# Experts of two layers: second products ahead of the next group's first, back transposes in the same step, the rows added by the experts

## The chip, the cores and the metric

The kernel runs on one core of one Trainium2 chip, in one launch. TensorE (PE in the profile, with PEld for its weight loads) multiplies, VectorE (DVE), ScalarE (ACT) and GpSimd (POOL) work on the results, and SyncE (SP) issues most DMAs. The metric is device time in microseconds (us); lower is better. Engines wait for each other by semaphores, and every wait and its order is written by hand.

## What is computed

Four transformer layers with normalisation behind each sum, on 16 sequences of 256 tokens of width 128, all in float32:

```python
x = _layernorm(x + _L0_attn_ref(x, ...), axis=-1)
x = _layernorm(x + _L0_ffn_ref(x, ...), axis=-1)    # 8 experts of width 512, each token takes 2
x = _layernorm(x + _L1_attn_ref(x, ...), axis=-1)   # one head, softmax over the queries
...
x = _layernorm(x + _L3_attn_ref(x, ...), axis=-1)   # linear attention
x = _layernorm(x + _L3_ffn_ref(x, ...), axis=-1)    # 16 experts, each token takes 1, capacity 320
```

In layer 0 a token's result is the sum of its two experts' outputs, each weighted by the softmax of the two router logits, so that the two weights add up to 1. In layer 3 a token goes to one expert, weighted by its probability; the tokens beyond an expert's 320 places get nothing from the layer, so that x alone is normalised.

## The kernel before

**Staging.** The stages follow each other: attention and routing of layer 0; the experts of layer 0; the combination of their results, in the same sweep as the attention of layer 1; mixing, attention, mixing; the linear attention and routing of layer 3; the experts of layer 3; the last stage, which combines, normalises and stores. The activations of all tokens stay on chip in `xg`.

**How a stage is ordered.** A stage is a `sweep(eng, lags, step)` on each engine. In step s, `at(k)` is the item s - k, so `at(0)` is the newest item and `at(3)` one that began three steps ago. On an engine the code runs in the order in which it is written. Items rotate through four slots (`q.slot`), some tiles through two. `wait_apart` waits for a semaphore; `q.back(3)` as a count says that item n - 4 is through.

**Experts (`experts_*`).** Tokens have been scattered into a table in memory, sorted by expert, each row with its destination row (column D) and its weight (column D + 1). An item is a group: 256 rows of one expert in layer 0 (T = 256, 40 groups), or one expert's 320 places in layer 3 (T = 320, 16 groups). SyncE loads its rows into `xe` (L1508; for T = 320 also L1511) and the expert's weights into `we` (L1478). On TensorE a step holds, in this order: the row transposes of item s (L1523, `xe` to `p0`), the first products of item s - 1 (L1530, four chunks into `pt` and `pm`), the second products of item s - 2 (L1536, four chunks into `po0`), and the back transposes of item s - 3 (L1543, `yt` to `po1`). ScalarE applies the GELU to each chunk of the first products (L1555, `he`). VectorE copies the transposed rows (L1569, `xet`), adds the bias (L1574, or a plain copy, L1577: `yt`), copies weight and destination (L1580 and L1581: `w_row`, `to_row`), and scales the result (L1589, `ye`). GpSimd scatters `ye` to memory with one indirect DMA for each 128 rows (L1613). The semaphores carry the names of the tiles: `he_ps` counts first products, `he_sb` GELUs, `yt_ps` second products, `ye_ps` back transposes.

**Behind the experts of layer 0.** Each token has two result rows. `combine_sync` waits for all scatters, then loads both for a sequence into `yr` (L1627, slot free when the sum of item s - 4 is made). `combine_vector` makes two sums (L1651: first result plus `xg`; L1655: plus the second result, into `mixed.res`), then the statistics (L319, L322); GpSimd takes the root (L328, L331, `norm_rstd`), and VectorE normalises into `xg` (L340). In the same steps, six items behind, VectorE does its part of layer 1's attention (`single_vector`); TensorE's part is `single_tensor`, whose products L796 wait for a normalisation by VectorE.

**Layer 3.** The linear attention leaves its normalised rows in `rows3`; SyncE copies them to `xg` on chip (L998), while GpSimd scatters them to the experts' table. The result table `yd3` in memory is filled with zeros early on (L1694), since dropped tokens have no result. The last stage loads one result row per token (L1627), adds `xg` (L1655), normalises and stores (L1664).

## Time and profile before

| | |
|---|---|
| three runs, median (lowest to highest) | 1377.04 us (1372.11 to 1378.55) |
| the profiled execution, whole | 1373.05 us |
| its span in the trace | 1371.3 us, granted TensorE clock 0.89 on average |
| busy share of the span | PE 79%, DVE 61%, ACT 47%, POOL 27% |
| experts of layer 0: first row transposes to the end of the last scatter | 362.4 to 530 us |
| combination of layer 0 with layer 1's attention | from 530.1 us |
| experts of layer 3: first row transposes to the end of the last scatter | 1232.4 to 1332 us |
| last stage | 1332 to 1371.3 us |

The shares are averages over stages of different kinds; what a change in one stage is worth is read from that stage: which engine has no idle time there, and which wait ends last. In a row of the trace that is ordered by time, the first number is the start, the second the duration (of all instructions of the row, if it ends in x2 or more), and in brackets the idle time before it with the engine and the tile that ended it. A float32 product counts as two MATMUL instructions.

### The profile page before, as it was taken

How to read it: one execution, taken by the hardware profiler on the slowest of the kernel's cores; microseconds unless marked ns; L12 is line 12 of the kernel's file. 1: busy time of each engine (PE TensorE's matmuls, PEld its weight loads, DVE VectorE, ACT ScalarE, POOL GpSimd, SP SyncE). 2: the span in 40 equal slices, each digit the busy share in tenths (PEclk: the TensorE clock that was granted, in tenths of full speed). 3: DMA queues.
4: the chain of work that ended last, by engine and by line, in shares of the span. 5: the costliest groups of instructions: out<-in, count | busy, mean ns of one | idle time of the engine just before them, and what ended most of it. 6: DMA issues, size and time to landing. Idle time of an engine off the chain costs nothing. (4 is left out here: it accounts for less than half of the span.)

```text
span 1371.3 us, 33015 instructions
## 1 busy us (share of the span) xinstructions
PE 1080.8 (79%) x9594; PEld 733.9 (54%) x9623; DVE 832.8 (61%) x3269; ACT 643.8 (47%) x1505; POOL 377.1 (27%) x602
## 2 busy tenths in 40 slices
PE   5989989886499994777779989998877798819950
PEld 2334444433388883676645545555566677716730
DVE  3788899985233334875645666667445677742327
ACT  2577777763344441554326656666633432204310
POOL 4012332235345444332200000000012133342554
PEclk9999999997699997999968999999999855559985
DMA  5222332312567677210032222221010011133523
GB/s 160 76 74 80 82 89 83 81 34 81 153 197 203 205 208 233 89 35 31 25 85 61 62 62 51 61 62 35 18 34 32 24 44 40 32 108 105 170 70 103
DMA packets 146579, 119.27 MB, mean 87 GB/s; under 512 B 16657, under 2 KB 134674, under 8 KB 146322
## 3 DMA queue, kind: packets, MB, share of 16 engines
q1 hardware_dynamic: 136912, 100.73, 25.8%
q0 software_dynamic: 7168, 14.37, 3.1%
q10 hardware_dynamic: 2370, 2.56, 0.7%
q8 instruction: 68, 1.11, 0.3%
q14 instruction: 61, 0.50, 0.1%
HBM read 47.26 MB, written 23.41 MB: 52 GB/s over the span
## 5 line engine op out<-in xcount | busy, mean ns | idle before, releaser
L655 DVE TENSOR_REDUCE mx<-pm 128x2 f32<-128x512 f32 (+1 forms) x512 | 304.8, 619 | 123.5 <-PE pm L450 74.2
L599 ACT ACTIVATE ex<-pt 128x512 f32<-128x512 f32 (+1 forms) x512 | 269.4, 547 | 163.4 <-PE pt L443 85.8
L328 POOL TENSOR_SCALAR ve<-mv 128x2 f32<-128x2 f32 x96 | 22.1, 230 | 661.3 <-DVE mv L322 660.8
L437 PE MATMUL pm<-ks,qs 64*128 64x256 bf16 (+1 forms) x1024 | 172.8, 259 | 8.3 <-DVE mx L655 5.2
L443 PE MATMUL pt<-qs,ks 64*128 64x256 bf16 (+1 forms) x1024 | 164.7, 250 | 0.6 <-ACT ex L599 0.3
L1613 POOL DMA_INDIRECT result<-ye,to_row x128 | 122.5, 957 | 151.6 <-issue 108.2
L474 PE MATMUL po<-ex,va 128*32 128x256 f32 (+1 forms) x2048 | 153.0, 371 | 6.0 <-issue 6.0
L437 PEld LDWEIGHTS pm<-ks,qs 64*128 64x128 bf16 x1024 | 74.2, 99 | 88.0 <-issue 53.4
L1536 PE MATMUL po<-he,we 128*128 128x256 f32 (+1 forms) x448 | 112.9, 395 | 0.6 <-DVE yt L1574 0.4
L424 PE MATMUL pm<-hide_q,half_id 64*128 64x256 bf16 (+1 forms) x512 | 89.1, 260 | 16.1 <-DVE mx L655 9.3
L1536 PEld LDWEIGHTS po<-he,we 128*128 128x128 f32 x448 | 85.0, 190 | 19.3 <-DVE yt L1574 0.6
L429 PE MATMUL pt<-hide_k,half_id 64*128 64x256 bf16 (+1 forms) x512 | 85.7, 252 | 1.3 <-ACT ex L599 0.9
L1574 DVE TENSOR_SCALAR yt<-po,we 128x256 f32<-128x256 f32 x40 | 19.4, 484 | 104.2 <-PE po L1536 104.2
L1555 ACT ACTIVATE he<-pt,we 128x256 f32<-128x256 f32 x80 | 36.1, 473 | 94.0 <-PE pt L1530 94.0
L443 PEld LDWEIGHTS pt<-qs,ks 64*128 64x128 bf16 x1024 | 70.6, 96 | 8.6 <-issue 6.7
L340 DVE TENSOR_SCALAR xg<-res,mv,rstd 128x128 f32<-128x128 f32 (+1 forms) x128 | 39.2, 349 | 56.6 <-POOL rstd L331 55.5
L1373 POOL DMA_INDIRECT sorted<-xr,place x64 | 63.8, 997 | 26.5 <-POOL xr L1367 13.4
L331 POOL TENSOR_TENSOR rstd<-ve,half 128x2 f32<-128x2 f32 x96 | 68.8, 717 | 8.0
L424 PEld LDWEIGHTS pm<-hide_q,half_id 64*128 64x128 bf16 x512 | 30.6, 96 | 74.5 <-issue 51.4
L311 ACT COPY xt<-p 128x256 f32<-128x256 f32 x96 | 35.4, 368 | 73.4 <-PE p L307 73.3
L1530 PE MATMUL pt<-xet,we 128*128 128x256 f32 (+1 forms) x224 | 64.8, 413 | 0.0
L1530 PE MATMUL pm<-xet,we 128*128 128x256 f32 (+1 forms) x224 | 62.5, 402 | 0.0
(294 smaller groups left out, 2460.4 us busy)
## 6 DMA issues: line engine op xcount, KB each, us to landing
we<-in_pack SPq DMA_DIRECT2D x40, 514.5 KB
xs<-xg SPq DMA_DIRECT2D x96, 128.0 KB, 2.0
qs<-parts SPq DMA_DIRECT2D x192, 64.0 KB
ks<-parts SPq DMA_DIRECT2D x192, 64.0 KB
we<-in_pack SPq DMA_DIRECT2D x16, 512.0 KB
xe<-sorted SPq DMA_DIRECT2D x56, 132.0 KB, 2.2
yr<-result SPq DMA_DIRECT2D x48, 128.0 KB, 2.2
xr<-xg SPq DMA_DIRECT2D x32, 128.0 KB, 2.3
```

The lines of the kernel that those rows point to most:

```text
L331: nc.gpsimd.tensor_tensor(of.rstd[q.slot][:, :, :], of.ve[q.slot][:, :, :], half[:, :].unsqueeze(2), ALU.pow).then_inc(of.ln_rs, 1)
L424: pe.matmul(dst, half_id[rows_m, lo // HALF, :], hide_q[rows_m, lo // HALF:lo // HALF + 1, lo:P].to_broadcast([HALF, 2, P - lo]), start=fi ...
L429: pe.matmul(dst, half_id[rows_t, 1 - lo // HALF, :], hide_k[rows_t, 1 - lo // HALF:2 - lo // HALF, 0:P - lo].to_broadcast([HALF, 2, P - lo ...
L437: last_m = pe.matmul(mine[:, e * S + k0:e * S + k1], queries, keys[:, k0:k1], start=not causal, stop=e == 1 or not causal)
L443: last_t = pe.matmul(theirs[:, e * S + k0:e * S + k1], keys, queries[:, k0:k1], start=not causal, stop=e == 1 or not causal)
L474: last = pe.matmul(po[32 * i:32 * i + 32, b // 2, c0 + lo:c0 + S], va[q.slot][:, kt, 4 * b + i, :], ex[j % 2][:, i, lo:S], start=(kt == 0) ...
L599: nc.scalar.activation(ex[j % 2][:, :, :].rearrange("p (e g) k -> p g e k", g=2)[:, 1 - u, :, lo:S], pt[:, u, :].rearrange("p (b k) -> p b ...
L655: nc.vector.tensor_reduce(mx[q.slot % 2][:, qt, u, 2 * b:2 * b + 2], pm[:, u, :].rearrange("p (b k) -> p b k", k=S)[:, :, 0:hi], AX.X, ALU ...
L1373: pool.indirect_dma_start(out=rows, out_offset=bass.IndirectOffsetOnAxis(ap=place[q.slot][:, i, t:t + 1], axis=0), in_=tile[:, t, :], in_o ...
L1530: pe.matmul(hb[c][:, 0:T], we[q.slot][:, c * P:c * P + P], xet[q.slot % 2][:, 0:T], start=True, stop=True).then_inc(he_ps, 1)
L1536: last = pe.matmul(po0[:, 0:T], we[q.slot][:, W2_AT + c * D:W2_AT + c * D + D], he[q.slot % 2][:, c, 0:T], start=(c == 0), stop=(c == FC - 1))
L1613: pool.indirect_dma_start(out=rows, out_offset=bass.IndirectOffsetOnAxis(ap=to_row[q.slot][0:m, i:i + 1], axis=0), in_=ye[q.slot][0:m, i, ...
```

## The change

- **Order on TensorE.** A step of the experts is now: row transposes of item s, second products of item s - 2, first products of item s - 1, back transposes of item s - 2. So the second products come ahead of the next group's first, and their results are transposed back in the same step; every engine's sweep has three lags in place of four.
- **The experts add the rows.** The scatter no longer writes the scaled result alone. In layer 3, `ye` becomes x + weight * result, in one operation for each 128 rows; in layer 0 it becomes 0.5 * x + weight * result in two operations on 256 rows, since each token has two rows that are summed. `w_row` goes: the weight is read from `xe`. Since `xe` is read until `ye` is made, the load of new rows waits for `ye_sb` instead of `to_row_sb`.
- **Combination.** In layer 0 one sum of the two result rows is left. In layer 3 SyncE writes the normalised rows of the linear attention to `yd3` in place of `xg`, and the scatters of the experts overwrite the rows of the tokens that were kept (GpSimd waits for those writes); the fill with zeros goes. The last stage loads each sequence's rows from `yd3` straight into `mixed.res` (`last_sync`), takes the statistics and normalises two steps later (`last_vector`), without a sum. The load of item s waits until item s - 4 is normalised.

```diff
@@ norm_stats
-        def norm_stats(dve, q, done, of=None, bank=None):
+        def norm_stats(dve, q, done, of=None, bank=None, loaded=False):
...
-            dve.wait_ge(of.res_sb, done + q.n + 1)
+            if not loaded:
+                dve.wait_ge(of.res_sb, done + q.n + 1)
@@ linear_sync
-                    sp.dma_start(xg[:, bass.ds(2 * q.n, 2), :], rows3[q.slot][:, :, 0:D]).then_inc(rows_moved[q.slot], 16)
+                    sp.dma_start(yd3[bass.ds(SPARE + q.n * S, S), :].rearrange("(t p) d -> p t d", p=P),
+                                 rows3[q.slot][:, :, 0:D]).then_inc(rows_moved[q.slot], 16)
@@ experts_sync
-                    wait_apart(sp, to_row_sb, a + q.back(3), passed)
+                    wait_apart(sp, ye_sb, a + q.back(3), passed)
@@ experts_tensor
                     last.then_inc(xet_ps, 1)
+                if (q := at(2)):
+                    wait(pe, yt_sb, a + q.n)
+                    pe.wait_ge(he_sb, 4 * (a + q.n + 1))
+                    for c in range(FC):
+                        last = pe.matmul(po0[:, 0:T], we[q.slot][:, W2_AT + c * D:W2_AT + c * D + D],
+                                         he[q.slot % 2][:, c, 0:T], start=(c == 0), stop=(c == FC - 1))
+                    last.then_inc(yt_ps, 1)
                 if (q := at(1)):
...
                 if (q := at(2)):
-                    wait(pe, yt_sb, a + q.n)
-                    pe.wait_ge(he_sb, 4 * (a + q.n + 1))
-                    for c in range(FC):
-                        last = pe.matmul(po0[:, 0:T], we[q.slot][:, W2_AT + c * D:W2_AT + c * D + D],
-                                         he[q.slot % 2][:, c, 0:T], start=(c == 0), stop=(c == FC - 1))
-                    last.then_inc(yt_ps, 1)
-                if (q := at(3)):
                     pe.wait_ge(yt_sb, a + q.n + 1)
                     wait(pe, ye_sb, a + q.n)
...
-            sweep(pe, 4, step, n, lead=0 if a else 1)
+            sweep(pe, 3, step, n, lead=0 if a else 1)
@@ experts_vector
                     for i, j, m in whole:
-                        nc.vector.tensor_copy(w_row[q.slot][0:m, i:j, :], xe[q.slot][0:m, i:j, D + 1:D + 2]).then_inc(w_row_sb, 1)
                         last = nc.vector.tensor_tensor(to_row[q.slot][0:m, i:j].unsqueeze(2), xe[q.slot][0:m, i:j, D:D + 1],
...
-                if (q := at(3)):
                     dve.wait_ge(ye_ps, a + q.n + 1)
-                    dve.wait_ge(w_row_sb, a + len(whole) * (q.n + 1))
                     wait(dve, grp_out[q.slot], outs + 16 * k * q.turn)
-                    for i, j, m in whole:
-                        last = nc.vector.tensor_tensor(ye[q.slot][0:m, i:j, :],
-                                                       po1[0:m, i * D:j * D].rearrange("p (t d) -> p t d", d=D),
-                                                       w_row[q.slot][0:m, i:j, :].to_broadcast([m, j - i, D]), ALU.mult)
+                    if biased:
+                        nc.vector.tensor_tensor(ye[q.slot][:, 0:2, :], po1[:, 0:2 * D].rearrange("p (t d) -> p t d", d=D),
+                                                xe[q.slot][:, 0:2, D + 1:D + 2].to_broadcast([P, 2, D]),
+                                                ALU.mult).then_inc(scaled_sb, 1)
+                        dve.wait_ge(scaled_sb, q.n + 1)
...
+                        last = nc.vector.scalar_tensor_tensor(ye[q.slot][:, 0:2, :], xe[q.slot][:, 0:2, 0:D], 0.5,
+                                                              ye[q.slot][:, 0:2, :], ALU.mult, ALU.add)
+                    else:
+                        for i, m in pieces(T):
+                            last = nc.vector.scalar_tensor_tensor(ye[q.slot][0:m, i:i + 1, :],
+                                                                  po1[0:m, i * D:i * D + D].unsqueeze(1),
+                                                                  xe[q.slot][0:m, i, D + 1:D + 2],
+                                                                  xe[q.slot][0:m, i:i + 1, 0:D], ALU.mult, ALU.add)
                     last.then_inc(ye_sb, 1)
@@ experts_pool
-                pool.wait_ge(zeroed, 48)
+                for s in rows_moved:
+                    pool.wait_ge(s, 48 * (SEQS // SLOTS))
...
-                if (q := at(3)):
+                if (q := at(2)):
@@ combine_vector
                 if (q := at(2)):
-                    dve.wait_ge(gathered[q.slot], got // SLOTS + 16 * choices * (q.turn + 1))
-                    src = xg[:, bass.ds(2 * q.n, 2), :]
-                    if choices == 2:
-                        nc.vector.tensor_tensor(part[q.slot % 2][:, :, :], yr[q.slot][:, :, 0, :], src,
-                                                ALU.add).then_inc(part_sb, 1)
-                        dve.wait_ge(part_sb, q.n + 1)
-                        src = part[q.slot % 2][:, :, :]
-                    nc.vector.tensor_tensor(mixed.res[q.slot][:, :, :], yr[q.slot][:, :, choices - 1, :], src,
+                    dve.wait_ge(gathered[q.slot], 32 * (q.turn + 1))
+                    nc.vector.tensor_tensor(mixed.res[q.slot][:, :, :], yr[q.slot][:, :, 0, :], yr[q.slot][:, :, 1, :],
                                             ALU.add).then_inc(mixed.res_sb, 1)
@@ store_out becomes last_sync
+            def step(at):
+                if (q := at(0)):
+                    wait_apart(sp, mixed.ln_x, 2 * (n + q.back(3)), passed)
+                    sp.dma_start(mixed.res[q.slot][:, :, :],
+                                 yd3[bass.ds(SPARE + q.n * S, S), :].rearrange("(t p) d -> p t d", p=P)
+                                 ).then_inc(gathered[q.slot], 16)
+                if (q := at(4)):
+                    wait_apart(sp, mixed.ln_x, 2 * (n + q.n + 1), passed)
                     sp.dma_start(out[bass.ds(2 * q.n, 2)].rearrange("t p d -> p t d"),
                                  xg[:, bass.ds(2 * q.n, 2), :]).then_inc(out_done, 16)
-            combine_sync(sp, n, 1, yd3, OUTS0 + OUTS3, 7, then)
+            sweep(sp, 5, step)
@@ last_vector (new)
+        def last_vector(dve, n, got):
+            def step(at):
+                if (q := at(0)):
+                    wait_apart(dve, gathered[q.slot], got // SLOTS + 16 * (q.turn + 1), passed)
+                    norm_stats(dve, q, n, mixed, loaded=True)
+                if (q := at(2)):
+                    norm_apply(dve, q, n, mixed)
+            sweep(dve, 3, step)
@@ sync block
-            sp.dma_start(yd3[SPARE:SPARE + SEQS * S, :].rearrange("n d -> (n d)").rearrange("(e p k) -> p e k", p=P, e=SEQS),
-                         zt[:, 0:2 * D].unsqueeze(1).to_broadcast([P, SEQS, 2 * D])).then_inc(zeroed, 16)
@@ vector block
-            for s in rows_moved:
-                dve.wait_ge(s, 48 * (N // SLOTS))
-            combine_vector(dve, N, 1, 32 * N)
+            last_vector(dve, N, 32 * N)
```

TensorE, before, the step that holds the first back transposes of layer 0's experts (`p0` to `po` are banks of results, `xe3` is slot 3 of the rows, `he1` of two the GELUs of item 1):

```order
L1523 MATMUL p0<-ident,xe3 128x128 [waits rows_in_sb3,xet_sb]
L1523 MATMUL p0<-ident,xe3 128x128
L1530 MATMUL pt<-xet0,we2 128x256 [waits he_sb,weights_in2,xet_sb]
L1530 MATMUL pt<-xet0,we2 128x256 [waits he_sb]
L1530 MATMUL pm<-xet0,we2 128x256 [waits he_sb] x2
L1536 MATMUL po<-he1,we1 128x256 [waits he_sb,yt_sb]
L1536 MATMUL po<-he1,we1 128x256 x3
L1543 MATMUL po<-ident,yt0 128x128 [waits yt_sb]
L1543 MATMUL po<-ident,yt0 128x128
```

TensorE, the same place in the change:

```order
L1523 MATMUL p0<-ident,xe2 128x128 [waits rows_in_sb2,xet_sb]
L1523 MATMUL p0<-ident,xe2 128x128
L1529 MATMUL po<-he0,we0 128x256 [waits he_sb]
L1529 MATMUL po<-he0,we0 128x256 x3
L1537 MATMUL pt<-xet1,we1 128x256 [waits he_sb,weights_in1,xet_sb]
L1537 MATMUL pt<-xet1,we1 128x256 [waits he_sb]
L1537 MATMUL pm<-xet1,we1 128x256 [waits he_sb] x2
L1543 MATMUL po<-ident,yt0 128x128 [waits yt_sb]
L1543 MATMUL po<-ident,yt0 128x128
```

The second products (`he0`) have moved ahead of the first products of the next group (`xet1`), and the back transposes of item 0 (`yt0`) follow one step earlier, behind the first products of item 1 instead of those of item 2.

SyncE, before, the last stage's loop (a load, then a store of another sequence):

```order
L1627 ISA [waits res_sb_m]
L1627 DMA yr2<-result3 128x2x128
L1663 ISA
L1664 ISA [waits ln_x_m]
L1664 DMA out_x<-xg 128x2x128
```

SyncE, the same loop in the change:

```order
L1668 ISA [waits ln_x_m]
L1668 DMA res_m0<-result3 128x2x128
L1673 ISA [waits ln_x_m]
L1673 DMA out_x<-xg 128x2x128
L110 ISA
```

The load now has `res_m` as its target and waits for `ln_x_m`, which counts normalisations, where it waited for `res_sb_m`, which counts sums.

## Rows read from the trace of the kernel before

**Rows 1.** Busy time by stretch: length; PE, PEld, DVE, ACT, POOL; clock, DMA share, GB/s

```profile
402.00:442.00 40.00, 40.00 (x208) 35.27 (x207) 13.19 (x51) 17.68 (x40) 20.31 (x21) 1.00 0.71 202
560.00:575.00 15.00, 11.08 (x75) 9.99 (x75) 13.82 (x54) 8.45 (x27) 5.74 (x13) 1.00 0.25 73
```

**Rows 2.** Order of time (start us, us, engine), one step in layer 0's experts

```profile
403.10 1.03 PE L1530 MATMUL pt<-xet,we 128*128 128x256 f32 x4
403.40 0.42 DVE L1589 TENSOR_TENSOR ye<-po,w_row 128x256 f32<-128x256 f32 x1
403.73 0.91 ACT L1555 ACTIVATE he<-pt,we 128x256 f32<-128x256 f32 x2 [2.12 <-PE pt L1530]
404.60 0.91 ACT L1555 ACTIVATE he<-pm,we 128x256 f32<-128x256 f32 x2
404.62 0.97 POOL L1613 DMA_INDIRECT result<-ye,to_row  x1 [1.65 <-issue]
404.83 1.89 PE L1536 MATMUL po<-he,we 128*128 128x256 f32 x8
406.55 0.38 PE L1543 MATMUL po<-ident,yt 128*128 128x128 f32 x2
406.99 1.03 PE L1530 MATMUL pt<-xet,we 128*128 128x256 f32 x4
```

**Rows 3.** Order of time, one step in layer 3's experts

```profile
1255.76 1.34 PE L1530 MATMUL pt<-xet,we 128*128 128x320 f32 x4
1257.68 1.07 ACT L1555 ACTIVATE he<-pm,zero_col 128x320 f32<-128x320 f32 x2
1258.02 2.32 PE L1536 MATMUL po<-he,we 128*128 128x320 f32 x8
1260.17 0.49 PE L1543 MATMUL po<-ident,yt 128*128 128x128 f32 x3
1261.02 1.34 PE L1530 MATMUL pt<-xet,we 128*128 128x320 f32 x4
```

**Rows 4.** Order of time, layer 0's last second products, which wait for yt

```profile
519.42 0.48 DVE L1574 TENSOR_SCALAR yt<-po,we 128x256 f32<-128x256 f32 x1 [2.72 <-PE po L1536]
519.96 1.99 PE L1536 MATMUL po<-he,we 128*128 128x256 f32 x8 [0.36 <-DVE yt L1574]
521.79 0.38 PE L1543 MATMUL po<-ident,yt 128*128 128x128 f32 x2
```

**Rows 5.** Order of time, the last scatter of layer 0's experts

```profile
527.72 0.96 POOL L1613 DMA_INDIRECT result<-ye,to_row  x1 [0.30 <-issue]
```

**Rows 6.** Loads of the experts' rows (xe): time from issue to landing

```profile
DMA to landing us min/median/max: 2.1/2.2/3.8
```

**Rows 7.** Order of time, the last stage: some sums, a load, the last normalisation

```profile
1334.12 0.43 DVE L1655 TENSOR_TENSOR res_m<-yr,xg 128x256 f32<-128x256 f32 x1 [10.97 <-DMA yr<-result]
1350.41 0.42 DVE L1655 TENSOR_TENSOR res_m<-yr,xg 128x256 f32<-128x256 f32 x1
1351.10 0.38 SPq L1627 DMA_DIRECT2D yr<-result  x1
1361.45 0.42 DVE L1655 TENSOR_TENSOR res_m<-yr,xg 128x256 f32<-128x256 f32 x1
1363.96 0.60 DVE L340 TENSOR_SCALAR xg<-res_m,mv_m,rstd_m 128x128 f32<-128x128 f32 x2 [0.75 <-POOL rstd_m L331]
```

**Rows 8.** Order of time, the end of layer 3's experts

```profile
1318.09 2.42 PE L1536 MATMUL po<-he,we 128*128 128x320 f32 x8 [0.25 <-DVE yt L1577]
1329.60 0.90 POOL L1613 DMA_INDIRECT result<-ye,to_row  x1 [0.30 <-issue]
```

**Rows 9.** Order of time, TensorE in layer 1's attention, one sequence to the next

```profile
593.23 0.71 PE L796 MATMUL po<-vn,e 128*128 128x128 f32 x4 [1.15 <-DVE xg L340]
598.47 0.68 PE L796 MATMUL po<-vn,e 128*128 128x128 f32 x4 [1.25 <-DVE xg L340]
603.69 0.68 PE L796 MATMUL po<-vn,e 128*128 128x128 f32 x4 [1.25 <-DVE xg L340]
```

More of the change, by code:

```diff
@@ L779, in post_norm_stack @@
             yr = [sb(f"yr{i}", [P, 2, 2, D], F32, mem) for i in range(SLOTS)]
-            part = [sb(f"part{i}", [P, 2, D], F32, mem) for i in range(2)]
         kq_ps, kq_sb, v1_ps, v1_sb = sem("kq_ps"), sem("kq_sb"), sem("v1_ps"), sem("v1_sb")
@@ L1449, in post_norm_stack @@
         xe = [sb(f"xe{i}", [P, 4, RW]) for i in range(SLOTS)]
-        w_row = [sb(f"w_row{i}", [P, 3, 1]) for i in range(SLOTS)]
         to_row = [sb(f"to_row{i}", [P, 4], U32) for i in range(SLOTS)]
@@ L1557, in step @@
                                              ).then_inc(he_sb, 1)
-            sweep(act, 4, step, n)
+            sweep(act, 3, step, n)
         def experts_vector(dve, a, T, n, biased):
@@ L1615, in step, with combine_sync @@
                             in_=ye[q.slot][0:m, i, :], in_offset=None).then_inc(grp_out[q.slot], 16)
-            sweep(pool, 4, step, n, lead=0 if a else SLOTS)
-        def combine_sync(sp, a, choices, rows, outs_done, lags, then):
+            sweep(pool, 3, step, n, lead=0 if a else SLOTS)
+        def combine_sync(sp, g):
             for s in grp_out:
-                sp.wait_ge(s, outs_done)
+                sp.wait_ge(s, OUTS0)
             def step(at):
                 if (q := at(0)):
-                    wait_apart(sp, mixed.res_sb, a + q.back(3), passed)
-                    for c in range(choices):
+                    wait_apart(sp, mixed.res_sb, q.back(3), passed)
+                    for c in range(2):
                         sp.dma_start(yr[q.slot][:, :, c, :],
-                                     rows[bass.ds(SPARE + c * SEQS * S + q.n * S, S), :].rearrange("(t p) d -> p t d", p=P)
+                                     yd0[bass.ds(SPARE + c * SEQS * S + q.n * S, S), :].rearrange("(t p) d -> p t d", p=P)
                                      ).then_inc(gathered[q.slot], 16)
-                then(at)
-            sweep(sp, lags, step)
+                if (q := at(4)):
+                    load_x(sp, q, g, "mixed")
+            sweep(sp, 5, step)
         def combine_pool(pool, a, then=None):
@@ L1780, in _ @@
             experts_vector(dve, 0, S, NG, True)
-            combine_vector(dve, 0, 2, 0, then=single_vector(dve, N))
+            combine_vector(dve, then=single_vector(dve, N))
             mixing_vector(dve, 0, 2 * N)
```

34 lines of the change are left out of this document (14 added, 20 removed).

## The prediction

> **What bounds the kernel now.** I read the busy time by stretch first, then the order of time inside one step of each stage that the change touches, and last the end of the program. In the experts of layer 0 (from 362 us to about 530 us) TensorE is busy for 40.00 of 40 us at full clock [rows 1]: it is the bound, so the step is what its instructions take. One step goes from a first product at 403.10 to the next at 406.99, 3.89 us [rows 2]: the first products take 1.73 (to 404.83), the second products 1.72 (to 406.55), and the two pairs of transposes 0.44 together. The experts of layer 3 are bound the same way, with 5.26 us (1255.76 to 1261.02) [rows 3]. The combination behind layer 0, which runs with the attention of layer 1, is another case: TensorE is busy for 11.08 of 15 us and VectorE for 13.82 [rows 1]. The last stage is VectorE's and the queues' alone.
>
> **Second products ahead of the next first products, layer 0.** The work on TensorE is the same; what changes is how long ScalarE has between a group's first and second products. Today a whole set of second products and more lies between. In the new order only two pairs of transposes do. First products start at w = 403.10; the first pair of GELUs starts at w + 0.63 and the second pair ends at 404.60 + 0.91 = w + 2.41 [rows 2]. One engine reacts to another's end within 0.06 us: yt ends at 519.42 + 0.48 and TensorE starts at 519.96 [rows 4]. So the second products may start at w + 2.47. TensorE would be ready for them at w + 1.73 + 0.44 = w + 2.17, and waits 0.30. Restarting costs more: the set that waited took 519.96 to 521.79 = 1.83 us [rows 4], against 1.72 in the stream, 0.11 more. Each step becomes 0.41 us longer (4.30). Nothing hides it, since TensorE is the bound. Of 40 groups 37 pay 0.41; the first and the last two, which have one pair of transposes less or a slow start before them, pay about 0.6. That is 15.2 + 1.8 = 17.0 us. At the start of the last second products the old order waits too, for yt: take off about 0.5; one pair of back transposes (0.22) now lies ahead of them, and the restart of that last set (0.11) is counted below: they start 16.6 us later.
>
> The end of the stage gives something back. Before, GpSimd's last scatter starts at 527.72, 7.76 us after the last second products [rows 4, 5], because it works off earlier groups back to back. Now: products 1.83, hand-over 0.2 (w + 0.63 less one product of 0.43), bias 0.48, transposes and hand-over 0.5, scaling and adding the rows 0.9 (one operation more of some 0.42, as the one of 403.40 [rows 2]), then 0.80 to GpSimd (403.40 + 0.42 to 404.62), and one scatter of 0.97 + 0.30: 6.0 us. Gain 1.8. Stage: **+14.8 us**.
>
> Moved with it in the same step: VectorE's extra operation and the lost copies of w_row lie in an engine that is busy for 13.19 of 40 us [rows 1], cost 0. The load of a group's rows now waits for ye instead of to_row. Counted from the start of the back transposes (b): ye ends near b + 1.4, the load lands 2.2 after its issue [rows 6], and the queue reacts by 0.27 (1350.41 + 0.42 to 1351.10, [rows 7]): b + 3.9. The row transposes stand at b + 4.5, and may slip to b + 4.7 since the second products wait anyway. Hidden, with 0.6 us of cover; behind that wait the queue holds the next weights, which are needed some 7 us later.
>
> **The same in layer 3.** First products last 2.26 (1255.76 to 1258.02), second 2.15, so both groups of transposes have 5.26 - 4.41 = 0.85. The last GELUs end at 1257.68 + 1.07 = w + 2.99, usable at w + 3.05; TensorE arrives at w + 3.11 [rows 3]. Cost 0 in the stream, with only 0.06 to spare; if it misses, 15 times 0.15 = 2 us at most. The end again gains: the last second products start at 1318.09 today [rows 8], and 0.9 later in the new order (0.33 for the transposes put ahead, two waits of 0.45 with 0.1 for a restart, less 0.4 of today's wait). Behind them: 2.26 + 0.75 to the back transposes, 0.55 and three operations of a quarter microsecond, 0.8 to GpSimd, two scatters of 1.27: 7.7 us, so the last scatter starts at 1326.7 instead of 1329.60 [rows 8]. **-2.9 us**. The three operations in place of two are bounded by 0.61 (the two of today) and 1.3 (three of 0.42).
>
> **Combination, layer 0.** One of two sums goes, 0.42 + 0.04 us on VectorE for each of 16 sequences, 7.3 us if VectorE's own time set the pace. It doesn't: with the sums the products of the attention start at 593.23 and 598.47 (5.24 apart), and where the sums have run out at 603.69 (5.22 apart), each time after 1.2 us of waiting for VectorE's normalisation [rows 9]. The pace is a ring through TensorE and back, and the sum lies beside it. Only at the start, where VectorE works alone, up to three sums are saved: 0 to 1.35 us; I take **-0.6**, the middle, as the queue there issues three transfers in each step. The zero fill of the result (one DMA) goes and the copy of the rows goes to memory instead of on chip; both end long before anyone waits: 0.
>
> **Last stage.** Today 16 sequences take 1334.12 to 1361.45, 1.82 each [rows 7], with the sum. Without it VectorE needs about 1.35 (1.82 less 0.46). But the rows are now loaded into the buffer that the normalisation still reads, so the load of sequence s waits until s-4 is normalised, and that stands in VectorE's step s-2. From there: 0.27 reaction (1350.41 + 0.42 to 1351.10), 2.2 to land [rows 6], then a step of 1.35. Two steps take 3.82, 1.91 each: **the wait for a load takes the place of the sum**. The first four sequences come from loads issued ahead and end 4.3 us after the first row is there; twelve more take 22.9; the last normalisation 1.4: 28.6 us. Today it is 1363.96 + 0.60 - 1334.12 = 30.4 [rows 7]. **-1.8 us**.
>
> **Sum.** +14.8 - 2.9 - 0.6 - 1.8 = +9.5 us. The profiled execution took 1373.05 us, so 1382.6 for one like it; the median of the three runs shown is 1377.04, 0.3% above it, and the change is small against that spread, so I put it on the median: 1386.5, say **1386**.
>
> **Clock.** In the stretch from 560 to 575 us TensorE idles 1.2 us in every 5.2 and the granted clock stays 1.00 (2.4 GHz) [rows 1], so pauses of 0.3 us in a step of 4.3 should leave it there. The Trainium skill (TensorE: Matmul & The Clock Gate, "A second HAM failure mode: psum-queue depth-cycling") says against this that frequent small pauses between groups of products can make the clock swing between its two levels. By that rule this reordering would be very dear, and the rows of this trace speak against it.
>
> **Rivals.**
> A, the other side: TensorE doesn't wait. If the GELUs were seen by w + 2.17, for which they would have to end 0.30 us earlier than in every step of the trace, the 17.0 us fall away: 9.5 - 17.0 = -7.5, 1369.5. What speaks for it is only that ScalarE is idle for half the time; against it, that its pace is that of the products. 10%.
> B, the row loads come late in layer 0. Landing takes 2.1 to 3.8 us [rows 6]; at 3.8 the rows are there at b + 5.5, 0.8 late. A quarter of the groups late costs 8 us (1394), all of them 30 us. 7%. The Trainium skill (DMA: Bandwidth & Descriptors, "Latency and other measured facts") gives access to HBM as 0.2 us on average and 2 us at high load; by the latter this rival would be the rule. The longest landing of the profile is 1.6 above the median, so it happens, if seldom.
> C, the sum that goes does pay in the combination: up to 16 x 0.46 = 7.3 instead of 0.6, 1379.8. It decides whether the wait before the normalisation begins with VectorE's queue or with TensorE's product. 12%.
> D, in the last stage loads and stores issued together land later, 2.9 instead of 2.2: six pairs of steps, +4.2, 1390.7. 11%.
> E, the clock falls in layer 0: at 1.2 GHz its 3.89 us of products a step double, over 100 us more. 1%.
> The forecast keeps 59%, from 1382 to 1390 with the spread of the runs.
>
> **Numbers.** 0.5% of 1377 is 6.9 us, about what a measurement of this kernel can tell from none. Faster by more: rival A, 8% (2% of it falls within). Within: 2% of A, C, and 16% of the forecast, 30%. Slower: the rest, 62%. The range leaves out A and the worst of B and E: 1376 to 1394.
>
> **What would show it.** In layer 0 TensorE's steps 4.3 us apart with about 0.3 idle before the second products, ended by ScalarE's he; 5.26 in layer 3 with none; the last scatter of layer 0 at about 542 us, some 14 us later; VectorE in the last stage waiting for the load from memory at every second sequence, 1.9 us apart. Steps of 3.9 mean A; TensorE waiting for the rows' DMA before the row transposes means B; products less than 5.1 us apart in the combination mean C. The forecast is wrong if ScalarE's turn is not on the path, or if the queue of the loads sets the step.

## The result and the profile after

The changed kernel takes 1379.69 us (median of 21 runs, 1373.17 to 1384.3) against 1373.88 us for the kernel before, run on the same chip with it (21 runs, 1367.71 to 1378.55): ratio 1.0043, 95% interval 1.003 to 1.0057. It is slower, by 5.8 us or 0.4%; the interval reaches just past 0.5%. The forecast was 1386 and "slower by over 0.5%"; the time lies in the range, the side doesn't. The profiled executions differ by 6.8 us: span 1378.1 after, 1371.3 before.

Where those 6.8 us arise can be followed with marks that both traces have. Each line below is the time from the mark of the line above to its own; the two columns on the right are the second profiled execution of either kernel, on another chip (experiments `g1` and `g2` below).

| stretch, us | before | after | difference | again: before | again: after |
|---|---|---|---|---|---|
| start to the first row transpose of layer 0's experts | 362.38 | 362.02 | -0.36 | 385.48 | 389.88 |
| from there to the end of the last second products | 159.57 | 175.63 | +16.06 | 160.20 | 175.35 |
| to layer 0's last scatter | 5.77 | 4.00 | -1.77 | 5.64 | 4.02 |
| to the last sequence's values in layer 1's attention (L871) | 90.18 | 88.62 | -1.56 | 90.13 | 88.17 |
| to the first row transpose of layer 3's experts | 614.53 | 612.02 | -2.51 | 620.52 | 610.22 |
| to layer 3's last scatter | 97.17 | 94.29 | -2.88 | 96.21 | 93.69 |
| to the end of the last normalisation | 34.96 | 34.83 | -0.13 | 35.11 | 34.55 |

In the first line and the fifth (mixing layers, layer 2, the linear attention of layer 3) the change touches only one fill with zeros and the target of a copy. The others together are +9.7 us, and in the second pair +8.5.

**Layer 0, one step.** Order of time in the changed kernel (start us, us, engine), the rows that answer to [rows 2]:

```profile
421.60 1.03 PE L1537 MATMUL pt<-xet,we 128*128 128x256 f32 x4
...
422.23 0.91 ACT L1555 ACTIVATE he<-pt,we 128x256 f32<-128x256 f32 x2 [2.52 <-PE pt L1537]
...
423.10 0.91 ACT L1555 ACTIVATE he<-pm,we 128x256 f32<-128x256 f32 x2
...
423.33 0.38 PE L1543 MATMUL po<-ident,yt 128*128 128x128 f32 x2
...
423.55 0.38 PE L1523 MATMUL p<-ident,xe 128*128 128x128 f32 x2
...
424.05 1.59 PEld L1529 LDWEIGHTS po<-he,we 128*128 128x128 f32 x8 [0.36 <-ACT he L1555]
424.05 1.99 PE L1529 MATMUL po<-he,we 128*128 128x256 f32 x8
...
425.88 1.03 PE L1537 MATMUL pt<-xet,we 128*128 128x256 f32 x4
```

From 421.60 to 425.88 is 4.28 us, against 3.89. The last GELU ends at 423.10 + 0.91 = 424.01, and 0.04 later the second products start; the weight load had been idle for 0.36. The set then takes 1.83 (424.05 to 425.88), where one in the stream took 1.72 [rows 2]. Busy time by stretch, the rows that answer to [rows 1] (length; PE, PEld, DVE, ACT, POOL; clock, DMA share, GB/s):

```profile
421.00:461.00 40.00, 38.85 (x188) 32.40 (x187) 16.34 (x47) 16.11 (x37) 18.39 (x20) 1.00 0.62 182
574.00:589.00 15.00, 11.99 (x78) 10.79 (x78) 12.63 (x50) 8.29 (x28) 6.03 (x12) 1.00 0.26 82
```

TensorE is no longer busy all the time, and the granted clock stays 1.00 (2.4 GHz) through a pause of 0.36 us in every step. The swing between two clock levels that the Trainium skill describes for another kernel (TensorE: Matmul & The Clock Gate, "A second HAM failure mode: psum-queue depth-cycling") doesn't occur here.

**The ends of both expert stages** (order of time; they answer to [rows 4, 5] and to [rows 8]):

```profile
535.68 1.97 PE L1529 MATMUL po<-he,we 128*128 128x256 f32 x8 [0.44 <-ACT he L1555]
...
541.65 0.96 POOL L1620 DMA_INDIRECT result<-ye,to_row  x1 [0.30 <-issue]
...
1336.58 0.90 POOL L1620 DMA_INDIRECT result<-ye,to_row  x1 [0.31 <-issue]
```

Layer 0's last second products start 15.72 later than before, its last scatter 13.93 later, and 5.97 after those products, against 7.76. In layer 3 the step is unchanged, as these rows show (first products, GELU, second products without a wait, next first products, 5.25 apart):

```profile
1310.05 1.24 PE L1537 MATMUL pt<-xet,we 128*128 128x320 f32 x4
...
1311.87 1.06 ACT L1555 ACTIVATE he<-pm,zero_col 128x320 f32<-128x320 f32 x2
...
1313.08 2.39 PE L1529 MATMUL po<-he,we 128*128 128x320 f32 x8
...
1315.30 0.97 PE L1537 MATMUL pt<-xet,we 128*128 128x320 f32 x3
```

**The last stage**, order of time on SyncE's queue and VectorE; it answers to [rows 7]:

```profile
1353.70 0.39 SPq L1673 DMA_DIRECT2D out_x<-xg  x1
...
1354.47 0.38 SPq L1668 DMA_DIRECT2D res_m<-result  x1
...
1355.12 0.49 DVE L320 BATCH_NORM_STATS2 st_m<-res_m 128x6 f32<-128x128 f32 x2 [1.01 <-DMA res_m<-result]
...
1355.95 0.60 DVE L341 TENSOR_SCALAR xg<-res_m,mv_m,rstd_m 128x128 f32 x2
...
1356.71 0.49 DVE L320 BATCH_NORM_STATS2 st_m<-res_m 128x6 f32<-128x128 f32 x2 [0.16 <-DMA res_m<-result]
1356.81 0.38 SPq L1668 DMA_DIRECT2D res_m<-result  x1
...
1359.02 0.49 DVE L320 BATCH_NORM_STATS2 st_m<-res_m 128x6 f32<-128x128 f32 x2 [0.88 <-DMA res_m<-result]
```

The chain that was forecast is there: a normalisation ends at 1355.95 + 0.60 = 1356.55, the load that waits for it leaves at 1356.81, and VectorE, which has waited 0.88, takes its statistics at 1359.02. Two sequences take 3.90, 1.95 each.

**What the change doesn't touch.** Nearly three microseconds come from a place that the prediction never looks at, the gate of layer 3 in the linear-attention layer. Four steps of that layer are the body of a loop that VectorE runs twice; its branches stand at 1133.5 us (back, for the second pass) and 1171.7 (out). The copy below is the first instruction of the second pass. Order of time, first before, then after:

```profile
1133.22 0.40 DVE L322 BATCH_NORM_AGGREGATE mv<-st 128x2 f32<-128x6 f32 x2
1136.69 0.19 DVE L1226 COPY lg<-pm 128x32 f32<-128x32 f32 x1 [3.07 <-issue]
...
1137.03 0.66 PE L1031 MATMUL pm<-tok,upto 128*128 128x64 f32 x2 [2.80 <-DVE lg L1226]
```

```profile
1146.05 0.40 DVE L323 BATCH_NORM_AGGREGATE mv<-st 128x2 f32<-128x6 f32 x2
1146.77 0.19 DVE L1227 COPY lg<-pm 128x32 f32<-128x32 f32 x1 [0.32 <-issue]
```

"issue" says that the engine waited for nothing that the profile shows. Before, it did so for 3.07 us, after for 0.32. TensorE waits 2.80 for that copy, so the pause is on the path: from the instruction that writes one sequence's `qt` (L1163 before, L1164 after) to the next one, the step that holds it takes 11.82 us before (1130.17 to 1141.99) and 9.06 after (1143.01 to 1152.07). Around it, queues and packets of the kernel before between 1132 and 1138 us (queue, kind: packets, MB, share of the engines):

```profile
q1 hardware_dynamic: 416, 0.26, 14.6%
q0 software_dynamic: 32, 0.07, 3.4%
q14 instruction: 3, 0.02, 1.3%
```

Three packets of instructions, 8 KB each, run in those six microseconds. In the changed kernel there is none between 1138 and 1151 us.

### The profile page after: what moved, and what is told of

Same layout as the page of the kernel before. It is cut to its first block, busy times and chain, and to the rows that moved or that the text cites. A ratio compares the mean times of both kernels' runs of the same rounds, so it can differ in the third digit from the quotient of the medians.

```text
span 1378.1 us, 33009 instructions
## 1 busy us (share of the span) xinstructions
PE 1099.6 (80%) x9623; PEld 734.7 (53%) x9623; DVE 844.1 (61%) x3221; ACT 643.6 (47%) x1505; POOL 374.7 (27%) x602
## 4 chain that ended last, share of the span: by engine, by line
PE 51%; DVE 18%; issue 11%; POOL 9%; ACT 5%; DMA 3%; SPq 1%; DVEq 1%; POOLq 0%; ACTq 0%
PE po L1529 9%; PE po L475 5%; DVE mx L656 4%; PE pm L438 4%; PE pt L1537 4%; PE pm L1537 4%; POOL rstd L332 3%; PE pm L425 3%; DVE xg L341 3%; POOL sorted L1374 3%; PE p L394 3%; ACT he L1555 2%; PE p L537 1%; DVE st L320 1%; PE p L515 1%
## 5 line engine op out<-in xcount | busy, mean ns | idle before, releaser
L1529 PE MATMUL po<-he,we 128*128 128x256 f32 (+1 forms) x448 | 118.6, 407 | 6.8 <-ACT he L1555 2.0
L1529 PEld LDWEIGHTS po<-he,we 128*128 128x128 f32 x448 | 80.7, 190 | 31.7 <-ACT he L1555 14.0
L475 PEld LDWEIGHTS po<-ex,va 128*32 128x32 f32 x2048 | 40.8, 109 | 38.4 <-issue 21.6
```

The lines of the kernel that those rows point to most:

```text
L475: last = pe.matmul(po[32 * i:32 * i + 32, b // 2, c0 + lo:c0 + S], va[q.slot][:, kt, 4 * b + i, :], ex[j % 2][:, i, lo:S], start=(kt == 0) ...
L1529: last = pe.matmul(po0[:, 0:T], we[q.slot][:, W2_AT + c * D:W2_AT + c * D + D], he[q.slot % 2][:, c, 0:T], start=(c == 0), stop=(c == FC - 1))
```

## The experiments

They ran on three other chips, on which the kernel before takes 1400 to 1402 us. The 27 us more lie in the attention of layer 0 and what comes before it (the first line of the table), where the profiles of the experiments are 23 to 33 us longer, whatever the kernel. The other stretches repeat to 1 us or better, half of them to 0.3, except the fifth, which scatters by up to 6. So each experiment is read by its ratio to the kernel before on its own chip, and by its stretches.

### One part alone: the order (f1_order)

```
 (kernel before; experts_tensor)
+                if (q := at(2)):          # second products, ahead of the first ones
+                    ...
                 if (q := at(1)):          # first products
                     ...
-                if (q := at(2)):          # second products
-                    ...
-                if (q := at(3)):          # transposes back
+                if (q := at(2)):
 (experts_vector and experts_pool: ye and the scatter at(2) instead of at(3); no rows added)
```

> The kernel before with one part of the change alone: on TensorE the second products stand ahead of the first ones and the results are transposed back in the same step, and VectorE and GpSimd scatter each group one step earlier; the rows aren't added in the experts, both combination sums and the last stage stay as before. Theory 1 (the order costs layer 0 its step: TensorE waits at the second products for the GELU of the group whose first products have only just ended): step of layer 0 4.28 to 4.30 us against 3.89, with a pause of 0.36 us ahead of the second products in each; the last second products of layer 0 15 to 16 us later than before; in layer 3 the step stays 5.26 and the stage ends about 3 us sooner, being one step shorter. Time 10 to 12 us over the kernel before: 1385. Theory 2 (it is the extra VectorE operation of adding the rows, or the rows being held longer, that stretches the step): step 3.89 to 3.95 here, last second products within 2 us of before, time within 3 us of the kernel before or below it by layer 3's 3 us: 1371.

Measured: 1409.87 us, ratio 1.0077 (1.0045 to 1.0109), 10.8 us. Order of time in its layer 0:

```profile
456.47 1.03 PE L1537 MATMUL pt<-xet,we 128*128 128x256 f32 x4
...
457.97 0.91 ACT L1555 ACTIVATE he<-pm,we 128x256 f32<-128x256 f32 x2
...
458.92 1.59 PEld L1529 LDWEIGHTS po<-he,we 128*128 128x128 f32 x8 [0.36 <-ACT he L1555]
...
460.76 1.03 PE L1537 MATMUL pt<-xet,we 128*128 128x256 f32 x4
```

The step is 4.29 with the same pause of 0.36, and layer 0 takes 175.26 us to its last second products, as in the changed kernel (175.63 and 175.35). Adding the rows on VectorE and holding them longer cost nothing there. Layer 3 to its last scatter takes 93.4 us, 3.7 less than the 97.2 before; that gain too belongs to the order.

### The wait split by chunk (f2_chunks)

```
-                    pe.wait_ge(he_sb, 4 * (a + q.n + 1))
                     for c in range(FC):
+                        pe.wait_ge(he_sb, 4 * (a + q.n) + c + 1)
                         last = pe.matmul(po0[:, 0:T], ...
```

> The changed kernel with one wait split: ahead of the four second products TensorE waits no longer for all four GELU chunks of the group but, ahead of each product, for the chunk that it reads. Theory 1 (the 0.36 us a step in layer 0 are the wait for the last chunk's GELU alone): the first chunk is ready by 0.4 to 1.3 us before TensorE comes to it, the last product begins 1.5 us after the first, so no pause is left; step 4.28 - 0.36 = 3.92 us, last second products of layer 0 38 x 0.36 = 13.7 us sooner than in the changed kernel, layer 3 as there (step 5.26); time 1379.7 - 13.7 = 1366, 8 below the kernel before. Theory 2 (behind the wait stands another limit of the new order, as the loads of rows held until the adding is done, or the products back from VectorE): the pause moves to the transposes or the first products, step 4.1 to 4.29, time 1373 to 1380.

Measured: 1392.38 us, ratio 0.9925 (0.9891 to 0.996), 9 us below the kernel before by the medians, 10.5 by the ratio. Its step (the weight load of the second products no longer waits):

```profile
462.74 1.60 PEld L1529 LDWEIGHTS po<-he,we 128*128 128x128 f32 x8
...
462.85 1.89 PE L1529 MATMUL po<-he,we 128*128 128x256 f32 x8
...
464.58 0.38 PE L1537 MATMUL pt<-xet,we 128*128 128x256 f32 x1
```

Second products 1.73 (462.85 to 464.58), no pause; the step is 3.89 again (the first products before these start at 460.69, 3.89 before 464.58), and layer 0 takes 159.29 us. It saves 16.3 us against the changed kernel, not the 13.7 expected: with the pause the price of restarting goes as well, 0.39 a step in all. What was slow in the new order was not the order but the granularity of its one wait. With a wait for each chunk the second products may begin when one GELU of four is ready.

### The last stage's step turned round (f3_apply_first)

```
             def step(at):
+                if (q := at(2)):
+                    norm_apply(dve, q, n, mixed)
                 if (q := at(0)):
                     wait_apart(dve, gathered[q.slot], ...
                     norm_stats(dve, q, n, mixed, loaded=True)
-                if (q := at(2)):
-                    norm_apply(dve, q, n, mixed)
```

> The changed kernel with the last stage's VectorE step turned round: it applies the normalisation of sequence s-2 first and then takes the statistics of sequence s, so that the slot is free, and the load of s+2 leaves, one part step sooner. Theory 1 (VectorE waits for the loads there, 0.8 to 1.0 us in every second sequence, because a load leaves only when sequence s-4 is normalised and lands 2.0 to 2.3 us later): the waits for the loads go, pitch of the last stage from 1.95 to 1.6 us a sequence, now set by the two transfers that SyncE issues for each (0.75 us apart), stage 4 to 5 us shorter, time 1375. Theory 2 (the stage is set by SyncE's issues or by the transfers themselves): pitch 1.9 to 1.97, time 1379 to 1380, with the waits only moved from the statistics to the normalisation.

Measured: 1404.38 us, ratio 1.0028 (0.9992 to 1.0063). By itself that interval doesn't tell 1.0028 from the 1.0032 of the unchanged kernel; the stretch does. From the first statistics to the end of the last normalisation it takes 25.88 us, against 30.23 and 29.96. SyncE's issues in it, order of time:

```profile
1379.50 0.38 SPq L1668 DMA_DIRECT2D res_m<-result  x1
...
1380.30 0.39 SPq L1673 DMA_DIRECT2D out_x<-xg  x1
...
1381.07 0.38 SPq L1668 DMA_DIRECT2D res_m<-result  x1
...
1381.82 0.39 SPq L1673 DMA_DIRECT2D out_x<-xg  x1
...
1382.59 0.38 SPq L1668 DMA_DIRECT2D res_m<-result  x1
```

One transfer leaves every 0.75 to 0.80 us, each only half of that busy; a load and a store make 1.54 a sequence, and 1.9 in each fourth. From the fifth statistics to the sixteenth the mean is 1.61. VectorE still waits now and then (0.42 us ahead of 1381.77). Theory 1, with its size: 4.35 us.

### The sum with the own rows left out (f4_one_sum)

```
-                    if choices == 2:
-                        nc.vector.tensor_tensor(part[...], yr[...][:, :, 0, :], src, ALU.add)...
-                        ...
+                    src = yr[q.slot][:, :, 0, :] if choices == 2 else xg[...]
```

> The kernel before with one thing left out: in the combination after layer 0 the sum with the sequence's own rows isn't made (one VectorE operation of 0.42 us a sequence less; the two loaded expert results are added, so that the residual is missing from the result). Theory 1 (the ring between TensorE and VectorE covers the sum except at the start): the stage to the last product of the single-head layer 0.6 to 1.6 us shorter, time 1373. Theory 2 (VectorE is the bound there and each of the 16 sums counts): 16 x 0.45 = 7.3 us shorter, pitch between 566 and 618 us from 5.15 to 4.7, time 1366.6.

Measured: 1396.78 us, ratio 0.9975 (0.9944 to 1.0007); the interval includes 1, so again the stretch has to tell. From the last scatter of layer 0 to the last values of layer 1's attention it takes 88.2 us, against 90.2 and 90.1 before: 2.0 less, a little over the upper end of theory 1 and far from theory 2. Between 586 and 602 us its values are still 5.15 us apart:

```profile
586.20 0.42 DVE L871 TENSOR_TENSOR v<-pt,rowb 128x256 f32<-128x256 f32 x1
591.35 0.42 DVE L871 TENSOR_TENSOR v<-pt,rowb 128x256 f32<-128x256 f32 x1 [0.41 <-PE pt L818]
```

It gains 0.8 us ahead of the first values, 0.9 in the first four of the 15 steps (the fourth is 3.91 us long where that of the kernel before is 4.37) and 0.3 in the eighth (5.15 against 5.44). Both executions of the kernel before have these two long steps, and no kernel without the sum has them.

### Both kernels once more (g1_before_again, g2_after_again)

> The kernel before, unchanged, for a second profiled execution of it. In the first one the stretch from the last sequence of the single-head layer to the first rows of layer 3 (untouched by the change) took 614.5 us, against 611.1 to 613.5 in the changed kernel and four others; one VectorE pause of 3.07 us that no wait explains lies in it. Theory 1 (such pauses fall where they will, in any kernel): this stretch comes out anywhere from 611 to 614.5 and the pause is gone or elsewhere; the stretches that the change touches repeat to 0.3 us: layer 0 to its last second product 159.6, combination 72.9, layer 3 88.1, last stage 30.0. Theory 2 (they belong to the code of this kernel): 614.5 again, with the pause of 3.1 at the same line.

> The changed kernel, unchanged, once more beside the kernel before. The stretches that the change touches add up to 9.7 us more than in the kernel before by the two profiles (layer 0 +16.1 and its end -1.8, combination -1.2, layer 3 +0.9 and its end -3.7, last stage +0.2, the rest -0.8), yet the median was 5.8 more. Theory 1 (the 3 to 4 us between are the scatter of the untouched stretches): the ratio lies anywhere from 1.003 to 1.009, on this chip nearer to 1.007, and the touched stretches repeat to 0.3 us. Theory 2 (the changed kernel gains in untouched stretches each time): ratio 1.004 again and the untouched stretch of 612.0 again.

Measured: the kernel before against itself 1.0004 (0.9981 to 1.0028); the changed kernel 1406.34 us, ratio 1.0032 (1.0015 to 1.005), 4.5 us. The stretches are in the table. The kernel before has its pause again, at the same line:

```profile
1166.08 0.19 DVE L1226 COPY lg<-pm 128x32 f32<-128x32 f32 x1 [2.95 <-issue]
```

and the changed kernel has none. Both theories of `g1` were half right: the untouched stretch does scatter (614.53 and then 620.52 us; the first five steps of the linear attention alone take 6.6 more, which is not explained), but the pause is not scatter. It stands in both executions of the kernel before and in `f1` (2.95), and in none of the kernels derived from the changed one; nor in `f4`.

### Both mends (g3_both), and the stores on another queue (g4_act_stores)

`g3` has the edits of `f2` and `f3`. `g4` has in addition:

```
 (last_sync)
-                if (q := at(4)):
-                    wait_apart(sp, mixed.ln_x, 2 * (n + q.n + 1), passed)
-                    sp.dma_start(out[...], xg[...]).then_inc(out_done, 16)
 (ScalarE, behind experts_scalar of layer 3)
+                    wait_apart(act, mixed.ln_x, 2 * (n + q.n + 1), passed)
+                    act.dma_start(out[...], xg[...]).then_inc(out_done, 16)
```

> The changed kernel with both mends at once: in the experts TensorE waits ahead of each second product for the one GELU chunk that it reads, and in the last stage VectorE applies the normalisation ahead of the next statistics. Theory 1 (the two losses are apart and add): layer 0 159.3 us as with the first mend alone, last stage 25.9 as with the second alone; 7.6 + 4.3 = 12 us below the kernel before, ratio 0.991. Theory 2 (they don't add, as one sets the state in which the other starts): last stage over 28 or layer 0 over 165, ratio 0.994 or more.

> As both mends, and the last stage's stores of results are issued from ScalarE's queue, which has nothing to do there, and not from SyncE's between the loads. Theory 1 (with the turned step the last stage goes at SyncE's pace, a store and a load each 0.76 us apart = 1.52 us a sequence, which is what its rows show): the pitch falls to VectorE's own 1.37 us, last stage 25.9 - 14 x 0.15 = 23.8 us, 2 us less than both mends alone. Theory 2 (the transfers themselves are the limit, or the normalisation's scale from GpSimd): pitch stays at 1.5 and the last stage at 25.5 to 26.5.

Measured: `g3` 1387.17 us, ratio 0.9888 (0.9852 to 0.9924), layer 0 in 159.16 us and the last stage in 25.92. The two mends add. It is the fastest version by its median, 15.7 us below the kernel before by the ratio. `g4`: 1388.46 us, 0.9895 (0.9859 to 0.9932), which doesn't differ from `g3` in time; its last stage takes 24.24 us, 1.7 less. Once the first load has landed, VectorE waits for one only once in it, for 0.09 us, and where it runs without a gap a sequence takes 1.39 us:

```profile
1366.42 0.48 DVE L320 BATCH_NORM_STATS2 st_m<-res_m 128x6 f32<-128x128 f32 x2
...
1367.29 0.61 DVE L341 TENSOR_SCALAR xg<-res_m,mv_m,rstd_m 128x128 f32 x2
...
1367.81 0.48 DVE L320 BATCH_NORM_STATS2 st_m<-res_m 128x6 f32<-128x128 f32 x2
```

From the fifth statistics to the sixteenth the mean is 1.45 us a sequence, against 1.61 in `f3` and `g3`. So SyncE's queue, with stores between the loads, held those two back by 0.16 a sequence.

### Where the pause comes from (h1_after_pad, h2_before_pad)

What the kernels with the pause share is the place of that code in VectorE's program. By a count of the program (the traces don't show it) the loop of the linear attention ends at instruction 2855 in the kernel before and 2853 in `f1`; in the changed kernel, with fewer VectorE instructions ahead of it, at 2833, and in `f4` at 2839. `h1` and `h2` move it, with the same edit:

```
 (VectorE, ahead of linear_vector)
+            for _ in range(22):           # h2: 112, in the kernel before
+                dve.sem_inc(passed, 1)
             dve.wait_ge(wt_sb, 5 * N)
```

> The changed kernel with 22 VectorE instructions without work (each only counts up a semaphore that nobody waits on) ahead of the linear-attention layer, so that the end of that layer's loop stands again where it stands in the kernel before (instruction 2855 of VectorE's program; in the changed kernel 2833). In three executions with that end at 2853 or 2855 VectorE paused for 2.95 to 3.07 us at the first instruction behind the loop, with instruction loads running; in six executions of kernels with it at 2833 and in one with it at 2839 it did not. Theory 1 (the place of the code in the program decides the pause): the pause of 3 us comes back at the copy of the gate's logits behind the loop, the time goes up by up to 3 us against the changed kernel, ratio to the kernel before about 1.006. Theory 2 (something else in the kernels before makes it): no pause there, ratio 1.003 to 1.004.

> The kernel before with 112 such instructions at the same place, so that the loop's end stands at 2967, that is 128 further than in the variant with one sum, which had no pause. Theory 1 (place decides, and repeats each 128 instructions): no pause of 3 us behind the loop. Theory 2 (the kernel before has it wherever the code stands): pause of 3 us at the same line.

Measured: the pause is back in the changed kernel, and gone from the kernel before. The first row is `h1`'s, the second `h2`'s:

```profile
1177.36 0.19 DVE L1227 COPY lg<-pm 128x32 f32<-128x32 f32 x1 [3.34 <-issue]
```

```profile
1175.73 0.19 DVE L1226 COPY lg<-pm 128x32 f32<-128x32 f32 x1 [0.32 <-issue]
```

With the loop's end at 2853 or 2855 it stands in four executions of four, elsewhere in none of eight (six at 2833, one at 2839, one at 2967). Three more things in the traces go with it:

- **The branch.** In all twelve the copy with the pause is the first instruction behind the branch back. There it starts 0.41 us after the branch without the pause, 3.04 to 3.43 with it. Behind the branch out of the loop it starts 0.10 us after it in every one.
- **The packets.** In the four with the pause, three instruction packets of 8 KB run within 4 us of the copy; in the eight others none runs from 9 us before it to 4 us behind it.
- **The path.** The step that holds the pause takes 11.70 to 12.09 us in the four and 9.01 to 10.05 in the eight, so the pause reaches the time of the layer, 2 to 3 us of it.

`h1` takes 1409.33 us, ratio 1.0084 (1.0049 to 1.012), against 1.0032 for the kernel without the padding on another chip: 7 us, give or take 5. Some of it is the padding, which isn't free: ahead of the first instruction behind it VectorE is held for 1.51 us here (0.07 for each of 22), and for 10.23 in `h2` (0.09 for each of 112). Its fifth stretch is 617.21 us, 5 to 7 over the changed kernel's 612.02 and 610.22, which is about the same. `h2` ran once, in 1411.69 us, padding included; that says nothing of what the pause costs. What the runs show is that the pause and the packets come and go together with the place of the code. The new target of the copy of rows isn't the cause, since `f4` and `h2` keep the old one and have no pause. That VectorE waits for these instructions to be loaded is the likely cause, inferred and not tested. That it repeats each 128 instructions isn't shown by one case.

## Why the prediction was right or wrong

**The step of layer 0** (forecast: step 4.30, start of the last second products 16.6 later, stage +14.8). Measured: 4.28 to 4.29, 15.7 later, +14.3. The wait, its releaser and its 0.3 are as forecast, and `f1` and `f2` show the mechanism from both sides. A step costs 0.39, not 0.41. The end of the stage gives back 1.8, as forecast.

**Layer 3** (forecast: step 5.26 at no cost, end -2.9). Measured: 5.25 and -2.88. The 0.06 us to spare held. In the steady part TensorE did not wait for the GELU; it did at the first group (0.31 us) and at the last two (0.38), which have no row transposes ahead of them.

**Combination** (forecast -0.6, the middle of 0 to 1.35). Measured: -1.56, and -2.0 in the second pair and in `f4`. The ring covers the sum in its steady steps, so rival C fell, but this term was too small. At the start the sum is worth 1.3 to 1.7 us, the top of the forecast's bounds and over, not their middle; and "only at the start" misses the eighth step, inside the ring, with 0.3 more.

**Last stage** (forecast: 28.6 us, -1.8). Measured: 30.23, -0.2. The exchange of a sum for a wait was right and its pitch nearly so (1.91 forecast; from the fifth statistics at 1347.17 to the sixteenth at 1368.65 eleven steps of 1.95). Mis-sized was the start:

```profile
1341.18 0.49 DVE L320 BATCH_NORM_STATS2 st_m<-res_m 128x6 f32<-128x128 f32 x2 [7.92 <-DMA res_m<-result]
...
1343.84 0.60 DVE L341 TENSOR_SCALAR xg<-res_m,mv_m,rstd_m 128x128 f32 x2
...
1344.74 0.39 SPq L1668 DMA_DIRECT2D res_m<-result  x1
...
1347.17 0.49 DVE L320 BATCH_NORM_STATS2 st_m<-res_m 128x6 f32<-128x128 f32 x2 [1.39 <-DMA res_m<-result]
```

The fifth load can't leave before the first normalisation ends at 1344.44, so the fifth statistics begin 5.99 us after the first, not 4.3: +1.7. The pitch adds 0.4, and the end, 2.76 behind the last statistics, takes 0.5 off again.

**The sum.** +9.5 was forecast for what the change touches; the two pairs of profiles give +9.7 and +8.5. That it fits so well is partly luck: the combination and layer 0 came out 1.5 us below their terms and the last stage 1.6 above its own.

**The step that failed** is that the sum of the four stages was taken for the change of the whole: the rest of the program stands in it at nothing, without a reason. But the changed program is shorter on VectorE, and that moved a loop's branch off a place where it costs nearly 3 us: the step that holds it fell from 11.82 to 9.06, -2.8. `h1` and `h2` show that the place of the code brings the pause and takes it away. The mechanism is not among the rivals. In the first pair of profiles it makes nearly all of the way from +9.7 to +6.8.

The medians point the same way. Against the kernel before on their own chip, the two experiments that have the pause and a changed order (`f1`, `h1`) took 1 to 2 us more than their touched stretches (and, for `h1`, the padding) add up to; the seven without it (the changed kernel twice, `f2`, `f3`, `f4`, `g3`, `g4`) took 1 to 4 us less. Each of these differences is only as good as its interval, 2 to 5 us either way, and other steps of the linear attention scatter by as much as the pause: `f1`, which has it, takes 612.97 us for the fifth stretch, no more than kernels that don't. So how much of the missing 3.7 us (9.5 against 5.8) is the pause and how much is scatter stays open; about 3 is an estimate, from the two step lengths.

**The base.** The forecast of 1386 put the sum on the median of three runs, 1377.04. Over 21 runs the kernel before has 1373.88. Half of the 6.3 us by which the number was off is this. With the profiled execution as the base, which the prediction names (1382.6), it would have been 2.9 off. The base has no part in the missed side, which goes by the difference: 9.5 us is 0.7%, and 5.8 is 0.4%. The 30% for "within 0.5%" was too little, since the spread of three runs, 0.5%, was as large as the bound.

Of the rivals, A (no wait) and B (late rows) fell: the wait stands in each step, and no row transpose waits for its load in the stretches read, and those loads land in 2.1 to 2.4 us. C fell, with the size above. D (loads land later) fell: loads in the last stage land in 2.0 to 2.3 us. E fell, the clock is 1.00.

## What to carry to other kernels

When a step is reordered so that a consumer comes closer to its producer, look at what the wait counts: here one wait for four chunks cost 0.39 us in each step of layer 0, and with four waits for one chunk each that cost was gone, so that a change that lost 0.4% gained 0.75%. Where a load's buffer is freed inside the step that it feeds, free it first (4.3 us here for two blocks exchanged), and count how often one queue must issue. And put a small forecast on the profiled execution or on many runs, and keep a few microseconds open on either side for code that only moves.

## What the runs showed of the hardware

- A pause of 2.95 to 3.34 us at the first VectorE instruction behind a loop's branch back, in four executions of twelve, whose presence depends on the place of the code in that engine's program. Three instruction packets of 8 KB move beside it in those four, none in the eight others. 22 instructions without work bring it back.
- TensorE has one like it in all twelve: in layer 2's attention one of its branches lasts 3.3 to 4.2 us.
- An instruction that only counts up a semaphore takes VectorE 0.07 to 0.09 us (22 of them hold it for 1.51 us, 112 for 10.23).
- SyncE issues one transfer every 0.75 to 0.80 us when waits and semaphore counts stand between, although each issue is busy for 0.38. With the two transfers of a sequence on two engines' queues the stage goes at 1.45 us a sequence in the mean instead of 1.61.
- A pause of 0.36 us in every 4.28 leaves the granted clock at 1.00.
- Products that restart behind a wait of 0.36 us take 0.11 more for a set of eight (1.83 against 1.72), with the clock unchanged.
